# A graph-network edge pipeline on one core: t moves beside s in PSUM and lags z by a step, and the v picks are added as 128 columns

## The chip, the cores and the metric

One core of a Trainium2 chip. The time is the device time of one run of the kernel, in microseconds (us); the median of several runs counts.

## What is computed

The reference, cut to what matters. N = 6250 nodes, D = 64, E = 200,000 edges sorted by `dst`, NB = 8 basis values for each edge.

```python
h  = relu(layernorm(x))
p1 = tanh(h @ pp_W1 + pp_b1) @ pp_W2 + pp_b2
inter = concat(p1[src], p1[dst]) @ pi_W1 + pi_b1
inter = (inter @ pi_W2 + pi_b2) @ pi_W3              # [E, 64*8]
i1 = einsum('ecb,eb->ec', inter.reshape(E, 64, 8), edge_attr)
i1 = tanh(i1 @ ii_W1 + ii_b1) @ ii_W2 + ii_b2
out = x + segment_sum(i1, dst, 6250)
```

## The kernel before, in words

**Tables first.** A prologue of some 95 us makes two tables in HBM, `u_tab` (the part of `inter` that comes from `src`, fp32) and `v_tab` (the part from `dst`, as three bf16 pieces whose sum is the fp32 value), and folds the weights into `g_sb` and `w_out`.

**The edge loop.** Edges go in NG = 391 groups of 512 (4 tiles of 128). Since `dst` is sorted, a group's `dst` values lie in a window of W = 42 nodes. The branch `is_fast` holds this loop; the other branch isn't taken. A group g passes through these pieces of work:

- *gather*: POOL issues 4 indirect DMAs (L392) that bring 128 rows of `u_tab` each into `u_rows`, a ring of UR = 8 groups. Before group g it waits until `s_ready` has counted group g-8, whose slot it takes (L390).
- *window and places*: SP issues two DMAs, `loc_bc` (L334, place of each edge in the window, sent to 126 partitions) and `v_win` (L338, 42 rows of `v_tab` as 126 partitions), rings of VR = 4. L338 waits for `s_ready` of group g-4, L334 for `hot_t_ready` of group g-4.
- *hot_t* (DVE, L765): one-hot of the places, 126 x 512, bf16.
- *s* (PE): `place_rows` (L1017) transposes the gathered rows into `s_ps` (bank 4 or 5, 256 columns of fp32, alternating), and `add_v` (L1025) adds v by two matmuls of 64 weight columns (`v_win`), one for each half of the 128 partitions (`TWICE[j]`), 256 moving columns each. It ends with `s_ready`.
- *st* (ACT, L538): 4 activations copy `s_ps` to `st_sb` (`st_ready`).
- *spread* (PE, L1033): 16 matmuls of 24 rows spread the basis values into `spread_ps` (banks 0 to 3, `spread_ready`).
- *products* (DVE, L697): `o_sb` = st times spread, 128 x 2048 in one instruction (`o_ready`).
- *z* (PE, `z_group`, L1041): 8 fp32 matmuls of 64 weight columns, 256 moving columns (16 records), into bank 6 columns 0 to 255 (`z_ready`).
- *tanh* (ACT, L526): `z_ps` to `tt_sb` (`tt_ready`).
- *t* (PE, `t_transposes`, L1048): two fp32 transposes of `tt_sb` into `t_ps`, bank 6 columns 256 to 511 (`t_ps_ready`).
- *copy_t* (ACT, L529): `t_ps` to `t_sb`, 2 buffers (`t_ready`).
- *hot* (DVE, L818): one-hot, 128 x 168, ring HR = 4.
- *seg* (PE, L1085): 4 fp32 matmuls of 65 weight columns and 42 moving ones into bank 7 (`seg_ready`).
- *add* (DVE, L795): bank 7 is added into the window of `acc_all` (`acc_done`).

An epilogue of some 25 us multiplies `acc` by `w_out`, adds x and stores.

**The order is written out by hand.** In step n the engines do, in this order:

- PE (`step`, a loop over 8 unrolled steps): s(n), spread(n-1), z(n-2), seg(n-3), t(n-2). z(n-2) waits for `t_ready` of group n-3, since z and t share bank 6 (L1077). t(n-2) waits for `tt_ready` of the same group (L1089).
- ACT: st(n), tanh(n-2), copy_t(n-2).
- DVE: add(n-4), in some steps a part of the basis split (L723 to L736), `places` (L757) or `turn` (L745), then hot_t(n+1), hot(n-2), products(n-1).
- POOL: 4 gathers of group n+8 as soon as s(n) frees their slot. SP: the two window DMAs.

ACT, DVE, POOL and SP run fully unrolled programs.

Of the kernel before, what the change touches and what calls it, by code (L numbers as in the profile page):

```python
# [8 lines left out]
def program(nc, x, src, dst, edge_attr, pp_W1, pp_b1, pp_W2, pp_b2, pi_W1, pi_b1, pi_W2, pi_b2, pi_W3,  # L9
# [53 lines left out]
    with ctx:  # L63
# [31 lines left out]
        u_rows = sb("u_rows", [P, UR, TILES, D])  # L95
        v_win = sb("v_win", [3 * W, VR, D], bf16)
        loc_bc = sb("loc_bc", [P, VR, GE], bf16)
# [53 lines left out]
        s_ps = [bank[4][:, 0:2 * P], bank[5][:, 0:2 * P]]  # L151
        z_ps, t_ps = bank[6][:, 0:2 * P], bank[6][:, 2 * P:2 * P + TILES * D]
        seg_ps = bank[7][0:D + 1, 0:W]
# [103 lines left out]
        def has(g):  # L257
            return 0 <= g < NG
# [3 lines left out]
        def _(sp):  # L262
# [57 lines left out]
            with sp.If(is_fast):  # L320
                for n in range(NG):
                    if has(n):
# [13 lines left out]
                        if g >= VR:  # L336
                            sp.wait_ge(s_ready, g - VR + 1)
                        sp.dma_start(v_win[:, g % VR, :], v_tab[bass.ds(start, W), :, :].rearrange("n w d -> w n d")  # L338
                                     ).then_inc(v_in[g % VR], 16)
# [17 lines left out]
        def _(pool):  # L357
# [13 lines left out]
            nc.gpsimd.memset(b_parts[:], 0.0)  # L371
            nc.gpsimd.memset(t_sb[:], 1.0)
            nc.gpsimd.memset(basis[:, FULL * NBT:], 0.0)
            nc.gpsimd.memset(src_e[:, FULL * TILES:], 0)
# [41 lines left out]
        def _(act):  # L416
# [111 lines left out]
            def copy_t(r):  # L528
                return nc.scalar.copy(t_sb[:, r, :, 0:D].rearrange("p (h q) c -> p q h c", h=2),  # L529
                                      t_ps.rearrange("p (q h c) -> p q h c", q=2, h=2))  # L530

# [10 lines left out]
            with act.If(is_fast):  # L542
                for n in STEPS:
                    if has(n):
                        act.wait_ge(s_ready, n + 1)
                        if has(n - 2):
                            act.wait_ge(o_ready, n - 1)
                        copy_st(n % 2).then_inc(st_ready, 1)
                    if has(n - 2):
                        g = n - 2  # L550
                        act.wait_ge(z_ready, g + 1)
                        if g >= 2:
                            act.wait_ge(t_ps_ready, g - 1)
                        tanh_z(g % 2).then_inc(tt_ready, 1)
                        act.wait_ge(t_ps_ready, g + 1)
                        if g >= 2:
                            act.wait_ge(seg_ready, g - 1)
                        copy_t(g % 2).then_inc(t_ready, 1)
            with act.Else():
# [11 lines left out]
        def _(dve):  # L571
# [203 lines left out]
            with dve.If(is_fast):  # L775
# [9 lines left out]
                for n in STEPS:  # L785
                    if n == 4:
                        dve.wait_ge(acc_zero, 1)
                    if has(n - 4):
                        g = n - 4
                        start = dve.value_load(base_row[0:1, g:g + 1], min_val=0, max_val=N - W)  # L790
# [100 lines left out]
        def _(pe):  # L891
# [130 lines left out]
            def add_v(u):  # L1022
                picks = hot_t[:, u % 2, :].rearrange("w (q j p) -> w j q p", q=2, j=2)
                for j in range(2):
                    last = nc.tensor.matmul(s_ps[u % 2][TWICE[j], :].rearrange("k (q p) -> k q p", q=2),  # L1025
                                            v_win[:, u % VR, :], picks[:, j], start=False, stop=True)
                return last
# [18 lines left out]
            def t_transposes(r):  # L1046
                for q in range(2):
                    last = nc.tensor.transpose(t_ps[:, q * P:(q + 1) * P], tt_sb[:, r, q * P:(q + 1) * P], ident[:])  # L1048
                return last

            def step(n, u, first, last_pass):
# [8 lines left out]
                if of(0):  # L1060
                    if of(2):
                        pe.wait_ge(st_ready, seen(2))
                    pe.wait_ge(u_in[u], n * (64 // UR) + 64)
                    place_rows(u_rows[:, u, :, :], u % 2, False)
                    pe.wait_ge(v_in[u % VR], n * (16 // VR) + 16 * (u // VR + 1))
                    pe.wait_ge(hot_t_ready, seen(0))
                    add_v(u).then_inc(s_ready, 1)
                if of(1):
                    if (u - 1) % BT == 0:
# [4 lines left out]
                if of(2):  # L1074
                    pe.wait_ge(o_ready, seen(2))
                    if of(3):
                        pe.wait_ge(t_ready, seen(3))  # L1077
                    z_group(u % 2).then_inc(z_ready, 1)
                if of(3):
                    pe.wait_ge(t_ready, seen(3))  # L1080
                    pe.wait_ge(hot_ready, seen(3))
                    if of(4):
                        pe.wait_ge(acc_done, seen(4))
                    for j in range(TILES):
                        last = nc.tensor.matmul(seg_ps, t_sb[:, (u - 3) % 2, j, :], hot[:, (u - 3) % HR, j, :],  # L1085
                                                start=(j == 0), stop=(j == TILES - 1))
                    last.then_inc(seg_ready, 1)
                if of(2):
                    pe.wait_ge(tt_ready, seen(2))  # L1089
                    t_transposes(u % 2).then_inc(t_ps_ready, 1)  # L1090

# [59 lines left out]
```

## Time and profile before

| what | value |
|---|---|
| three runs: median (lowest to highest) | 2601.27 us (2601.23 to 2613.06) |
| the profiled execution: its own time / its span | 2618.32 us / 2616.5 us |
| mean granted TensorE clock, share of 2.4 GHz | 0.814 |
| busy: PE, weight loads, DVE, ACT, POOL | 71%, 45%, 53%, 41%, 58% |
| DMA | 125.86 MB, 48 GB/s |

The span is what the trace shows from the first to the last instruction, and 1.8 us of the execution's own time lie outside it. A matmul's start is recorded and its end is modelled, so the time at which another engine is released tells when a matmul was really known to be complete. "remote" as releaser means that a wait ended by a semaphore for which the profile found no instruction that had ended just before.

### The profile page before, as it was taken

How to read it: one execution, taken by the hardware profiler on the slowest of the kernel's cores; microseconds unless marked ns; L12 is line 12 of the kernel's file. 1: busy time of each engine (PE TensorE's matmuls, PEld its weight loads, DVE VectorE, ACT ScalarE, POOL GpSimd, SP SyncE). 2: the span in 40 equal slices, each digit the busy share in tenths (PEclk: the TensorE clock that was granted, in tenths of full speed). 3: DMA queues.
4: the chain of work that ended last, by engine and by line, in shares of the span. 5: the costliest groups of instructions: out<-in, count | busy, mean ns of one | idle time of the engine just before them, and what ended most of it. 6: DMA issues, size and time to landing. Idle time of an engine off the chain costs nothing.

```text
span 2616.5 us, 52109 instructions
## 1 busy us (share of the span) xinstructions
PE 1864.1 (71%) x18378; PEld 1177.1 (45%) x18378; DVE 1383.5 (53%) x2286; ACT 1070.9 (41%) x2409; POOL 1521.1 (58%) x1581
## 2 busy tenths in 40 slices
PE   4277777677777767767677767777777767777777
PEld 3144444444444444444444444444444444444445
DVE  5354555555555545545555555455455554555555
ACT  4144444344444444444444444444444433444444
POOL 2666566566566665565666566666556655566660
PEclk8578878888778788788887887887777877887878
DMA  3322222222222222222222122222222122222221
GB/s 104 68 49 46 47 49 43 47 49 45 48 43 48 48 46 48 46 44 48 48 45 49 43 48 48 46 48 49 44 46 50 43 48 41 48 45 43 45 44 38
DMA packets 311278, 125.86 MB, mean 48 GB/s; under 512 B 233399, under 2 KB 283433, under 8 KB 311161
## 3 DMA queue, kind: packets, MB, share of 16 engines
q1 hardware_dynamic: 259985, 73.19, 14.1%
q0 software_dynamic: 50048, 51.35, 10.4%
q14 instruction: 105, 0.86, 0.1%
q10 hardware_dynamic: 1128, 0.26, 0.1%
q8 instruction: 12, 0.20, 0.0%
HBM read 118.67 MB, written 6.00 MB: 48 GB/s over the span
## 4 chain that ended last, share of the span: by engine, by line
PE 59%; issue 16%; another core or an unknown queue 14%; ACT 7%; DVE 2%; SPq 1%; ACTq 0%; DVEq 0%; DMA 0%
PE bank L1041 34%; PE bank L1048 6%; PE bank L1085 6%; PE spread_ps L1033 4%; PE bank L1025 4%; ACT st_sb L538 4%; PE bank L1017 3%; ACT tt_sb L526 2%; DVE o_sb L697 1%; SPq L277 0%; ACT t_sb L529 0%; PE spread_ps L1125 0%; PE bank L921 0%; DMA v_tab<-acc_all 0%
## 5 line engine op out<-in xcount | busy, mean ns | idle before, releaser
L392 POOL DMA_INDIRECT u_rows<-u_tab,src_e x1564 | 1514.7, 968 | 1034.8 <-PE bank L1025 476.8
L1041 PE MATMUL bank<-o_sb,g_sb 128*64 128x256 f32 x6256 | 1025.7, 484 | 284.8 <-issue 232.2
L697 DVE TENSOR_TENSOR o_sb<-st_sb,spread_ps 128x2048 f32<-128x2048 f32 x391 | 891.3, 2280 | 234.5 <-PE spread_ps L1033 134.0
L1041 PEld LDWEIGHTS bank<-o_sb,g_sb 128*64 128x64 f32 x6256 | 569.8, 171 | 580.0 <-issue 458.5
L538 ACT ACTIVATE st_sb<-bank,s_bias 64x256 f32<-64x256 f32 x1564 | 734.1, 469 | 117.6 <-PE bank L1025 83.2
L795 DVE TENSOR_TENSOR acc_all<-acc_all,bank 65x42 f32 x391 | 76.1, 195 | 919.0 <-remote 640.3
L526 ACT ACTIVATE tt_sb<-bank,z_bias 128x256 f32<-128x256 f32 x391 | 185.5, 474 | 753.0 <-PE bank L1041 386.6
L1048 PE MATMUL bank<-ident,tt_sb 128*128 128x128 f32 x782 | 188.2, 326 | 366.7 <-ACT tt_sb L526 234.4
L529 ACT COPY t_sb<-bank 128x256 f32<-128x256 f32 x391 | 146.5, 375 | 618.8 <-remote 340.8
L1085 PEld LDWEIGHTS bank<-hot,t_sb 128*65 128x65 f32 x3128 | 247.5, 156 | 210.4 <-issue 209.5
L1085 PE MATMUL bank<-hot,t_sb 128*65 128x42 f32 x3128 | 298.0, 251 | 10.8 <-issue 10.2
L1048 PEld LDWEIGHTS bank<-ident,tt_sb 128*128 128x128 f32 x782 | 88.9, 157 | 405.9 <-ACT tt_sb L526 255.4
L1017 PE MATMUL bank<-ident,u_rows 128*128 128x128 f32 x782 | 171.7, 306 | 21.0 <-issue 17.1
L1033 PE MATMUL spread_ps<-bt_sb,spread 24*128 24x128 bf16 x6256 | 171.9, 232 | 7.0 <-DVE o_sb L697 4.8
L765 DVE TENSOR_SCALAR hot_t<-loc_bc,iota_p 126x512 bf16<-126x512 bf16 x391 | 148.6, 380 | 20.7 <-DMA loc_bc<-loc_tab 19.0
L1025 PE MATMUL bank<-hot_t,v_win 126*64 126x256 bf16 x782 | 127.4, 323 | 32.0 <-DMA v_win<-v_tab 27.8
L1033 PEld LDWEIGHTS spread_ps<-bt_sb,spread 24*128 24x128 bf16 x6256 | 98.5, 98 | 63.5 <-issue 19.2
L818 DVE TENSOR_TENSOR hot<-loc_e,iota_f 128x168 f32<-128x168 f32 x391 | 125.6, 321 | 0.0
L1017 PEld LDWEIGHTS bank<-ident,u_rows 128*128 128x128 f32 x782 | 109.2, 158 | 32.0 <-issue 31.7
L1025 PEld LDWEIGHTS bank<-hot_t,v_win 126*64 126x64 bf16 x782 | 44.5, 111 | 110.4 <-issue 81.6
L757 DVE TENSOR_TENSOR loc_e<-dst_e,start_bc 32x16 f32<-32x16 int32 (+1 forms) x400 | 71.3, 178 | 8.7 <-issue 3.7
L745 DVE STREAM_TRANSPOSE bt_sb<-b_parts 128x512 bf16<-128x512 bf16 x98 | 68.8, 702 | 0.0
(109 smaller groups left out, 227.7 us busy)
## 6 DMA issues: line engine op xcount, KB each, us to landing
loc_bc<-loc_tab SPq DMA_DIRECT2D x391, 126.0 KB
u_rows<-u_tab,src_e POOLq DMA_INDIRECT x1564
v_win<-v_tab SPq DMA_DIRECT2D x391, 15.8 KB
basis<-edge_attr SPq DMA_DIRECT2D x24, 256.0 KB
v_tab<-acc_all SPq DMA_DIRECT2D x6, 375.0 KB
u_tab<-basis SPq DMA_DIRECT2D x6, 250.0 KB
out<-x_sb SPq DMA_DIRECT2D x2, 750.0 KB
x_sb<-x SPq DMA_DIRECT2D x3, 375.0 KB
```

What stands on the lines that cost most here:

```text
L392: pool.indirect_dma_start(out=u_rows[:, g % UR, j, :], out_offset=None, in_=u_tab[:, :], in_offset=bass.IndirectOffsetOnAxis(ap=src_e[:, g ...
L526: return nc.scalar.activation(tt_sb[:, r, :], z_ps, ACT.Tanh, bias=z_bias[:, 0:1])
L529: return nc.scalar.copy(t_sb[:, r, :, 0:D].rearrange("p (h q) c -> p q h c", h=2), t_ps.rearrange("p (q h c) -> p q h c", q=2, h=2))
L538: last = nc.scalar.activation(tiles[h * D:(h + 1) * D, j], s_ps[r][part].rearrange("p (q a e) -> p q a e", q=2, a=TILES), ACT.Identity, bi ...
L697: return nc.vector.tensor_tensor(o_sb[:, r, :, :].rearrange("p c (j e) -> p j c e", j=TILES), st_sb[:, r, :].rearrange("p (j e) -> p j e", ...
L765: nc.vector.tensor_scalar(hot_t[:, g % 2, :], loc_bc[0:3 * W, g % VR, :], iota_p[0:3 * W, 0:1], None, ALU.is_equal).then_inc(hot_t_ready, 1)
L1017: last = nc.tensor.matmul(s_ps[r][:, q * P:(q + 1) * P], rows[:, 2 * q:2 * q + 2, :].rearrange("p j k -> p (j k)"), ident[:], start=(q == ...
L1025: last = nc.tensor.matmul(s_ps[u % 2][TWICE[j], :].rearrange("k (q p) -> k q p", q=2), v_win[:, u % VR, :], picks[:, j], start=False, stop ...
L1033: last = nc.tensor.matmul(spread_ps[:, a, c * P:(c + 1) * P], spread[q, 2 * c:2 * c + 2, :].rearrange("p b k -> p (b k)"), bt_sb[q, r, :], ...
L1041: last = nc.tensor.matmul(z_ps[h * D:(h + 1) * D, 0:2 * P], g_sb[:, c, :], o_sb[:, r, c, 2 * h * P:(2 * h + 2) * P], start=(c == 0), stop= ...
L1048: last = nc.tensor.transpose(t_ps[:, q * P:(q + 1) * P], tt_sb[:, r, q * P:(q + 1) * P], ident[:])
L1085: last = nc.tensor.matmul(seg_ps, t_sb[:, (u - 3) % 2, j, :], hot[:, (u - 3) % HR, j, :], start=(j == 0), stop=(j == TILES - 1))
```

## The change

Three things change in the fast branch.

1. `t_ps` gets two buffers, in the upper 256 columns of banks 4 and 5, beside the two of s. It leaves bank 6 to z alone.
2. The order: PE does in step n s(n), t(n-3), seg(n-4), spread(n-1), z(n-2); ACT st(n), copy_t(n-3), tanh(n-2); DVE adds group n-5. z(n-2) now waits for `tt_ready` of group n-3 in place of `t_ready`. Since t(n-3) writes the bank from which st(n-1) was read, it waits for `st_ready` of n-1, and s(n) waits for `t_ready` of n-4 (the bank that copy_t read).
3. `v_win` is three times as wide, with zeros left and right of v (a memset of POOL in the prologue). `add_v` takes 128 weight columns, [v, 0] for one j and [0, v] for the other, and both matmuls write all 128 partitions.

```diff
-        v_win = sb("v_win", [3 * W, VR, D], bf16)
+        v_win = sb("v_win", [3 * W, VR, 3 * D], bf16)
-        z_ps, t_ps = bank[6][:, 0:2 * P], bank[6][:, 2 * P:2 * P + TILES * D]
+        z_ps = bank[6][:, 0:2 * P]
+        t_ps = [bank[4][:, 2 * P:4 * P], bank[5][:, 2 * P:4 * P]]
...
-                        sp.dma_start(v_win[:, g % VR, :], v_tab[bass.ds(start, W), :, :].rearrange("n w d -> w n d")
+                        sp.dma_start(v_win[:, g % VR, D:2 * D], v_tab[bass.ds(start, W), :, :].rearrange("n w d -> w n d")
...
+            nc.gpsimd.memset(v_win[:], 0.0)
...
+                    if has(n - 3):
+                        g = n - 3
+                        act.wait_ge(t_ps_ready, g + 1)
+                        if g >= 2:
+                            act.wait_ge(seg_ready, g - 1)
+                        copy_t(g % 2).then_inc(t_ready, 1)
                     if has(n - 2):
                         g = n - 2
                         act.wait_ge(z_ready, g + 1)
                         if g >= 2:
                             act.wait_ge(t_ps_ready, g - 1)
                         tanh_z(g % 2).then_inc(tt_ready, 1)
-                        act.wait_ge(t_ps_ready, g + 1)
-                        if g >= 2:
-                            act.wait_ge(seg_ready, g - 1)
-                        copy_t(g % 2).then_inc(t_ready, 1)
...
-                    if has(n - 4):
-                        g = n - 4
+                    if has(n - 5):
+                        g = n - 5
...
                 for j in range(2):
-                    last = nc.tensor.matmul(s_ps[u % 2][TWICE[j], :].rearrange("k (q p) -> k q p", q=2),
-                                            v_win[:, u % VR, :], picks[:, j], start=False, stop=True)
+                    last = nc.tensor.matmul(s_ps[u % 2].rearrange("k (q p) -> k q p", q=2),
+                                            v_win[:, u % VR, (1 - j) * D:(3 - j) * D], picks[:, j],
+                                            start=False, stop=(j == 1))
...
                 if of(0):
                     if of(2):
                         pe.wait_ge(st_ready, seen(2))
+                    if of(4):
+                        pe.wait_ge(t_ready, seen(4))
...
+                if of(3):
+                    pe.wait_ge(tt_ready, seen(3))
+                    if of(1):
+                        pe.wait_ge(st_ready, seen(1))
+                    if of(5):
+                        pe.wait_ge(t_ready, seen(5))
+                    t_transposes((u - 3) % 2).then_inc(t_ps_ready, 1)
+                if of(4):
+                    pe.wait_ge(t_ready, seen(4))
+                    pe.wait_ge(hot_ready, seen(4))
+                    if of(5):
+                        pe.wait_ge(acc_done, seen(5))
+                    for j in range(TILES):
+                        last = nc.tensor.matmul(seg_ps, t_sb[:, (u - 4) % 2, j, :], hot[:, (u - 4) % HR, j, :],
+                                                start=(j == 0), stop=(j == TILES - 1))
+                    last.then_inc(seg_ready, 1)
...
                 if of(2):
                     pe.wait_ge(o_ready, seen(2))
                     if of(3):
-                        pe.wait_ge(t_ready, seen(3))
+                        pe.wait_ge(tt_ready, seen(3))
                     z_group(u % 2).then_inc(z_ready, 1)
-                if of(3):
...
-                if of(2):
-                    pe.wait_ge(tt_ready, seen(2))
-                    t_transposes(u % 2).then_inc(t_ps_ready, 1)
```

## Rows read from the trace of the kernel before

**Rows 1.** The page: busy time of the engines, and the chain that ended last.

```profile
PE 1864.1 (71%) x18378; PEld 1177.1 (45%) x18378; DVE 1383.5 (53%) x2286; ACT 1070.9 (41%) x2409; POOL 1521.1 (58%) x1581
...
PE 59%; issue 16%; another core or an unknown queue 14%; ACT 7%; DVE 2%; SPq 1%; ACTq 0%; DVEq 0%; DMA 0%
```

**Rows 2.** The waits: engine, line, releaser, us in total, times, longest.

```profile
DVE acc_all L795 <- remote: 640.3, 214, 4.1
POOL u_rows L392 <- PE bank L1025: 476.8, 264, 7.9
...
ACT t_sb L529 <- remote: 340.8, 138, 3.2
...
PE bank L1048 <- ACT tt_sb L526: 234.4, 160, 7.4
...
PE bank L1041 <- ACT t_sb L529: 52.0, 45, 2.5
```

**Rows 3.** One line's duration (ns min/median/max), first and last start, by line.

```profile
L1041 PE MATMUL bank<-o_sb,g_sb x6256: 379/379/690, 106.5 to 2592.5; 128*64 128x256 f32 x196
...
L392 POOL DMA_INDIRECT u_rows<-u_tab,src_e x1564: 939/945/2692, 50.1 to 2556.1; - x196
```

**Rows 4.** Timeline of a plain step: start, us, engine, line, count, idle before and releaser.

```profile
1428.12 1.92 ACT L538 ACTIVATE st_sb<-bank,s_bias 64x256 f32<-64x256 f32 x4
1428.14 0.95 POOL L392 DMA_INDIRECT u_rows<-u_tab,src_e  x1 [1.46 <-remote]
1428.37 1.95 PE L1041 MATMUL bank<-o_sb,g_sb 128*64 128x256 f32 x16 [1.71 <-issue]
...
1428.63 2.27 DVE L697 TENSOR_TENSOR o_sb<-st_sb,spread_ps 128x2048 f32<-128x2048 f32 x1
1429.39 0.94 POOL L392 DMA_INDIRECT u_rows<-u_tab,src_e  x1 [0.30 <-issue]
...
1430.24 0.67 PE L1085 MATMUL bank<-hot,t_sb 128*65 128x42 f32 x8
...
1431.77 0.47 ACT L526 ACTIVATE tt_sb<-bank,z_bias 128x256 f32<-128x256 f32 x1 [1.73 <-PE bank L1041]
1431.89 0.94 POOL L392 DMA_INDIRECT u_rows<-u_tab,src_e  x1 [0.30 <-issue]
1432.30 0.44 PE L1048 MATMUL bank<-ident,tt_sb 128*128 128x128 f32 x2 [1.39 <-issue]
1432.85 0.43 PE L1017 MATMUL bank<-ident,u_rows 128*128 128x128 f32 x2
1433.21 0.30 PE L1025 MATMUL bank<-hot_t,v_win 126*64 126x256 bf16 x2
1433.44 0.40 PE L1033 MATMUL spread_ps<-bt_sb,spread 24*128 24x128 bf16 x16
1434.01 0.37 ACT L529 COPY t_sb<-bank 128x256 f32<-128x256 f32 x1 [1.77 <-PE bank L1048]
1434.14 0.20 DVE L795 TENSOR_TENSOR acc_all<-acc_all,bank 65x42 f32 x1 [3.24 <-remote]
...
1434.31 0.95 POOL L392 DMA_INDIRECT u_rows<-u_tab,src_e  x1 [1.47 <-PE bank L1025]
```

**Rows 5.** Timeline where POOL issues eight gathers without a pause.

```profile
1484.30 1.22 POOL L392 DMA_INDIRECT u_rows<-u_tab,src_e  x1 [1.94 <-PE bank L1025]
...
1487.63 1.95 PE L1041 MATMUL bank<-o_sb,g_sb 128*64 128x256 f32 x16
...
1493.64 0.94 POOL L392 DMA_INDIRECT u_rows<-u_tab,src_e  x1 [0.30 <-issue]
1496.06 0.47 ACT L526 ACTIVATE tt_sb<-bank,z_bias 128x256 f32<-128x256 f32 x1 [6.18 <-remote]
```

**Rows 6.** Busy time by stretch: us, engines' busy us (instructions), clock, DMA share, GB/s.

```profile
1483.90:1487.60 3.70, 3.64 (x46) 2.37 (x46) 3.61 (x7) 2.62 (x7) 2.69 (x3) 1.00 0.18 40
1487.60:1498.50 10.90, 4.62 (x54) 2.81 (x46) 4.18 (x6) 3.12 (x7) 5.62 (x7) 0.85 0.16 37
...
1612.30:1620.30 8.00, 6.64 (x46) 4.06 (x46) 6.29 (x21) 2.92 (x7) 3.77 (x5) 0.50 0.21 44
```

**Rows 7.** Groups by line: engine, shapes, count, busy us, mean ns, idle before.

```profile
L1025 PE MATMUL bank<-hot_t,v_win 126*64 126x256 bf16 x782 | 127.4, 323 | 32.0 <-DMA v_win<-v_tab 27.8 <-DVE hot_t L765 4.2
...
L371 POOL MEMSET b_parts<- 128x4096 bf16 x1 | 3.5, 3507 | 0.0
```

More of the change, by code:

```diff
@@ L529, in copy_t @@
                 return nc.scalar.copy(t_sb[:, r, :, 0:D].rearrange("p (h q) c -> p q h c", h=2),
-                                      t_ps.rearrange("p (q h c) -> p q h c", q=2, h=2))
+                                      t_ps[r].rearrange("p (q h c) -> p q h c", q=2, h=2))
             def copy_st(r):
@@ L785, in _ @@
                 for n in STEPS:
-                    if n == 4:
+                    if n == 5:
                         dve.wait_ge(acc_zero, 1)
-                    if has(n - 4):
-                        g = n - 4
+                    if has(n - 5):
+                        g = n - 5
                         start = dve.value_load(base_row[0:1, g:g + 1], min_val=0, max_val=N - W)
@@ L1047, in t_transposes @@
                 for q in range(2):
-                    last = nc.tensor.transpose(t_ps[:, q * P:(q + 1) * P], tt_sb[:, r, q * P:(q + 1) * P], ident[:])
+                    last = nc.tensor.transpose(t_ps[r][:, q * P:(q + 1) * P], tt_sb[:, r, q * P:(q + 1) * P], ident[:])
                 return last
@@ L1076, in step @@
                     if of(3):
-                        pe.wait_ge(t_ready, seen(3))
+                        pe.wait_ge(tt_ready, seen(3))
                     z_group(u % 2).then_inc(z_ready, 1)
-                if of(3):
[L1080 to L1087, printed above, removed]
-                if of(2):
-                    pe.wait_ge(tt_ready, seen(2))
-                    t_transposes(u % 2).then_inc(t_ps_ready, 1)
             with pe.If(is_fast):
```

## The prediction

> **What bounds the kernel now.** I read the page first [rows 1]. No engine is full: PE 71%, POOL 58%, DVE 53%. The chain that ended last holds 14% of releases from nowhere. So the bound is a ring of waits, and the waits tell which [rows 2]. The largest come from PE to others (DVE's add 640 us, ACT's copy_t 341 us, both "remote"), then POOL waiting 477 us for s. PE's own wait for copy_t, the one that the change removes, is only 52 us in total.
>
> Then the length of a step: the records of z start between 106.5 and 2592.5 [rows 3], 390 steps of (2592.5-106.5)/390 = 6.37 us. Prologue and epilogue are the other 131 us of the span.
>
> Then one plain step [rows 4], and what it shows decides this prediction. seg is recorded from 1430.24 and should be over by 1430.91, but DVE's add, which waits for nothing else, starts at 1434.14, after 3.24 us of idle time. t is recorded over at 1432.74, copy_t starts at 1434.01. s and spread, issued after them, are released within the same 0.3 us. So the completions of seg, t, s and spread reach the other engines in one bunch, and the bunch comes 2.1 us after the start of the group's fourth gather (1431.89). POOL then sees s and starts the next four at 1434.31. Hence the ring: s released, four gathers 1.25 us apart (1428.14 to 1431.89), 2.1 us to the bunch, 0.3 us to POOL's restart: 3.75+2.1+0.3 = 6.15, against 1434.31-1428.14 = 6.17. Where POOL issues eight gathers in a row [rows 5] it is starker: z, recorded from 1487.63 for 1.95 us, is seen by tanh at 1496.06, 2.4 us after the start of the last gather (1493.64). The same step done while POOL paused took 3.70 us [rows 6]. I take it that gathers in flight hold back the news of finished matmuls; the trace shows the coincidence in every plain step I read (over half of the steps lie between 6.05 and 6.35 us), not the cause.
>
> **The change, part by part.** The sum is made against the profiled execution, 2618.3 us; the median of the runs is 17 us lower, and I take those off at the end.
>
> *copy_t out of z's way.* Now z starts at 1428.37, after copy_t's 0.37 us and some 0.15 us of hops [rows 4]. Afterwards z(n-2) waits for products(n-2) and tanh(n-3), both done by then, so it can follow spread directly at 1433.84 in place of 1434.44: up to 0.6 us a step earlier. If nothing held the news, that is at most 0.6x390 = 234 us. In a plain step it is worth nothing by itself: the ring of the gathers doesn't pass through z. z is then finished early in the gathers' next batch, when news still passes.
>
> *t and seg a step later.* t(n-2) used to wait for tanh right behind seg; now s(n+1) lies in between, some 0.7 us of work (L1017 and L1025) [rows 4]. Queued behind the waiting t are now seg, spread and z; before, t had s, spread and z behind it. s escapes, so POOL's and SP's DMAs hang on t no longer. That is the real gain: s(n+1) can be done about 2.9 us after the bunch. It needs copy_t(n-3), which on ACT lies behind st(n): 1.92+0.37 [rows 4], then s itself, 0.43+0.30 less overlap. Seen early, it lets POOL go on to eight gathers without pause. Eight gathers with their tail took 9.3+2.4 us, with the restart 12.0 for two steps: 6.0 each [rows 5]. So plain steps go from 6.17 to between 6.0 and 6.17.
>
> *The long steps.* The mean, 6.37, is above the plain step, since steps at half clock take 8.0 us (granted 0.50) and a step after a hurried one 10.9, 14.6 for the pair against 2x6.17 [rows 6]. They are made by PE's own order (z, tanh, t, s in series), so these are where the 0.6 us and s's freedom help. I take the mean down to about 6.10: below the plain step's 6.17, above the 6.0 of double batches. That is 0.27x390 = -105 us. Bounds: 0 and 0.37 us (6.37 to 6.0), 144 us.
>
> *add_v with 128 columns.* The two matmuls of 297 to 323 ns lie almost on each other today, 0.30 us for both [rows 4, 7], since each has half of the columns. Side by side no more, they take up to a second 0.30 less overlap; nearest row: 16 z records at 0.12 us each for 256 columns. I take +0.11 us of PE a step, covered by the held bunch (PE idles 1.71 us before z). If that cover went, 0.11x390 = 43 us; below, nothing.
>
> By the Trainium skill, "TensorE: Matmul & The Clock Gate", Part 3, matmuls on distinct column groups run concurrently, and 128 columns give that up; the rows agree with it.
>
> *Waits added.* t(n-3) waits for st(n-1), over one step earlier; s(n) for copy_t(n-4), done 3.5 us earlier or more in the plain step, but the tight one if ACT is late. DVE's add a step later: it had 3.24 us of idle time ahead [rows 4], nothing. One more step to drain at the end: +4 us (the 3.70 of the hurried step, [rows 6]). The memset on POOL: 768 elements at 3507 ns for 4096 [rows 7] is 0.7 us, under POOL's wait in the prologue (first gather at 50.1, [rows 3]). SP issues as many DMAs of the same pieces.
>
> Sum: 2618.3-105+4 = 2517, less 17: **2500 us**.
>
> **The rivals.**
>
> *A. The news isn't held by the gathers.* Then only engines and true waits bind: POOL needs 4x1.25 = 5.0 us a step, PE 3.7 and DVE 3.6 [rows 6]. The floor: 390x5.0 = 1950, and 131, and 2: 2083, less 17: about 2066; with some idle at half clock 2150. For it: one step did run in 3.70 us. Against it: that was when POOL paused, and the bunches keep step with the fourth gather, not with PE's work. Chance 0.13.
>
> By the Trainium skill, "SBUF — State Buffer", Who interferes with whom, PE and ACT never wait on anyone, DMA included; by that rule this rival's time would come out. Rows 5, with 6.18 us of held z, speak against reading it so.
>
> *B. No difference.* s(n+1) is seen only with the bunch, POOL's ring stays at 6.17, and half-clock steps stay long. What is gained in z is lost in the same wait. 2595 to 2610. Chance 0.15.
>
> *C. Slower: tanh behind st and copy_t, with spread and z behind t.* On ACT tanh(n-2) now lies behind st(n) and copy_t(n-3), and on PE spread(n) and z(n-1) lie behind t(n-2). If z's news comes with the bunch, the chain is st 1.92, copy_t 0.37, tanh 0.47, t 0.44, seg 0.67, spread 0.40, z 1.95 = 6.2 us, as long as the ring [rows 4]. At half clock PE's part (3.46) is nearly twice that, 6.1 to 6.9, and the chain 8.9 to 9.7 against 8.0 today [rows 6]. The mean clock of 0.814 says that some 0.37 of the time is at half clock. Then (0.9 to 1.7)x0.37 = 0.33 to 0.6 us a step: +130 to +240, 2730 to 2840; half of that if only part of these steps are hit, 2670. It decides where z's news is later than copy_t's end. For it: z's news did come with the bunch in rows 5. Against it: in the plain step tanh started 3.4 us after z's start, before the bunch. Chance 0.28.
>
> **How the numbers follow.** My forecast, a modest gain, has 0.44. Faster by over 0.5%: 0.44 less 0.02 for its edge, plus 0.13 for A: 0.55. Within 0.5% (what a measurement of this kernel can tell from no change): 0.16. Slower: 0.29. The forecast's own range is 2450 to 2590. To hold 8 in 10 I go down towards A without holding its floor (2300), and up through B and most of C (2710).
>
> **What would show it.** Right: z starts with no wait for copy_t (the 52 us are gone); copy_t and add still start in a bunch about 2.1 us after a group's last gather; more runs of eight gathers; a mean step near 6.1. Wrong towards A: POOL's wait for s falls to nearly nothing and steps reach 5.0 us. Wrong towards C: PE waits longer ahead of L1048, now with spread late behind it, and POOL's wait for s grows above 477 us.

## The result, and the profile after

| kernel | median us (lowest to highest), runs | ratio to before, 95% interval |
|---|---|---|
| before | 2603.14 (2601.23 to 2613.06), 4 | |
| after | 2711.26 (2709.42 to 2720.29), 4 | 1.0414 [1.0379, 1.045] |

The change costs 108 us. The forecast of 2500 us had the wrong sign; the time lies just above the range's end of 2710, between the half and the full price of rival C. The profiled execution of after took 2720.29 us.

The page of after, busy time and chain, beside [rows 1]:

```profile
PE 1917.7 (71%) x18378; PEld 1189.0 (44%) x18378; DVE 1361.3 (50%) x2286; ACT 1089.9 (40%) x2409; POOL 1517.3 (56%) x1582
...
another core or an unknown queue 38%; issue 20%; DVE 18%; PE 15%; DVEq 4%; ACT 3%; SPq 1%; ACTq 0%; DMA 0%
```

No engine does more that matters (PE +54 us, at nearly the same mean clock, 0.82). What grew is the share of the chain whose releaser the profile can't name, 14% to 38%, and DVE's, 2% to 18%. One line's duration, first and last start, beside [rows 3]:

```profile
L1047 PE MATMUL bank<-o_sb,g_sb x6256: 376/379/689, 105.0 to 2694.0; 128*64 128x256 f32 x196
```

z is now L1047, and a step takes (2694.0-105.0)/390 = 6.64 us against 6.37. From the first z to the last, after takes 2589.0 us and before 2486.0: 103 us more, which is all of the 102 us between the two profiled executions. The waits of after, beside [rows 2]:

```profile
DVE o_sb L702 <- remote: 1145.2, 324, 8.2
ACT tt_sb L529 <- remote: 629.8, 194, 6.5
...
PE bank L1054 <- ACT tt_sb L529: 502.1, 250, 4.7
POOL u_rows L395 <- PE bank L1030: 514.1, 227, 5.6
...
ACT st_sb L541 <- DVE o_sb L702: 285.1, 254, 1.9
```

DVE no longer waits in its add but in its products (L702), for spread: 1145 us in 324 steps. PE's wait for tanh ahead of t doubled, from 234 to 502 us. The groups by line of after (busy us, mean ns, idle us before) for seg (L1089), copy_t (L532), add (L800) and add_v (L1030):

```profile
L1089 PE MATMUL bank<-hot,t_sb 128*65 128x42 f32 x3128 | 301.8, 256 | 188.2 <-DVE acc_all L800 179.6 <-issue 0.3
...
L532 ACT COPY t_sb<-bank 128x256 f32<-128x256 f32 x391 | 146.9, 376 | 11.0 <-PE bank L1054 1.6
...
L800 DVE TENSOR_TENSOR acc_all<-acc_all,bank 65x42 f32 x391 | 73.4, 188 | 4.9 <-PE bank L1089 4.9
...
L1030 PE MATMUL bank<-hot_t,v_win 126*128 126x256 bf16 x782 | 165.8, 296 | 34.8 <-DMA v_win<-v_tab 27.8
```

The add (L800) had 640 us of remote wait ahead of it before [rows 2]; now it starts with none, because what it adds is ready long before DVE comes to it, and PE's seg waits 180 us for it instead. A step of after in its timeline (t is L1054, seg L1089, spread L1039, z L1047, s L1022 and L1030):

```profile
1415.57 0.40 PE L1039 MATMUL spread_ps<-bt_sb,spread 24*128 24x128 bf16 x16
...
1417.99 0.95 POOL L395 DMA_INDIRECT u_rows<-u_tab,src_e  x1 [0.30 <-issue]
...
1420.04 2.29 DVE L702 TENSOR_TENSOR o_sb<-st_sb,spread_ps 128x2048 f32<-128x2048 f32 x1 [3.49 <-remote]
1420.10 0.47 ACT L529 ACTIVATE tt_sb<-bank,z_bias 128x256 f32<-128x256 f32 x1 [2.95 <-remote]
...
1420.63 0.44 PE L1054 MATMUL bank<-ident,tt_sb 128*128 128x128 f32 x2 [2.19 <-ACT tt_sb L529]
...
1422.24 0.19 DVE L800 TENSOR_TENSOR acc_all<-acc_all,bank 65x42 f32 x1
...
1422.58 0.64 PE L1089 MATMUL bank<-hot,t_sb 128*65 128x42 f32 x8 [1.51 <-DVE acc_all L800]
...
1423.15 0.57 PE L1039 MATMUL spread_ps<-bt_sb,spread 24*128 24x128 bf16 x16
...
1423.65 3.42 PE L1047 MATMUL bank<-o_sb,g_sb 128*64 128x256 f32 x16
...
1426.26 2.29 DVE L702 TENSOR_TENSOR o_sb<-st_sb,spread_ps 128x2048 f32<-128x2048 f32 x1 [3.32 <-remote]
...
1426.99 0.44 PE L1022 MATMUL bank<-ident,u_rows 128*128 128x128 f32 x2
...
1428.40 0.97 POOL L395 DMA_INDIRECT u_rows<-u_tab,src_e  x1 [3.31 <-PE bank L1030]
```

Read it from the bunch at 1420.04, 2.05 us after the start of the last gather (1417.99), as in the kernel before. Spread, over at 1415.97, comes out only there, and so does z (tanh starts at 1420.10, with ACT idle for 2.95 us). From here PE works in its new order: t waits for tanh, seg waits for the add, the add stands on DVE behind products' 2.29 us, and only behind seg come spread (1423.15) and z (1423.65). In the kernel before, spread was done ahead of the bunch and z stood first behind it [rows 4]. So the next s comes late: it starts at 1426.99, 6.95 us after the bunch, and POOL, done with its four gathers, idles for 3.31 us up to 1428.40. Spread, over at 1423.72, is again seen only with the next bunch at 1426.26, so the next products start late too, and the loop closes.

Part of the length of this step is the clock: it was granted at 0.76 of full speed from 1420.04 to 1426.26, and z takes 3.42 us in place of 1.95. A step of the kernel before with z as slow is the fair one to hold beside it. These are its z and the s behind it:

```profile
1434.44 3.27 PE L1041 MATMUL bank<-o_sb,g_sb 128*64 128x256 f32 x16 [0.59 <-issue]
...
1438.55 0.38 PE L1017 MATMUL bank<-ident,u_rows 128*128 128x128 f32 x2
```

There s starts 4.54 us after copy_t showed the bunch (1434.01), 2.4 us sooner than in after.

### The profile page after: what moved, and what is told of

The parts are those of the page before. It is cut to its first block, busy times and chain, and to the rows that moved or that the text cites. A ratio compares the mean times of both kernels' runs of the same rounds, so it can differ in the third digit from the quotient of the medians.

```text
span 2718.5 us, 52595 instructions
## 1 busy us (share of the span) xinstructions
PE 1917.7 (71%) x18378; PEld 1189.0 (44%) x18378; DVE 1361.3 (50%) x2286; ACT 1089.9 (40%) x2409; POOL 1517.3 (56%) x1582
## 4 chain that ended last, share of the span: by engine, by line
another core or an unknown queue 38%; issue 20%; DVE 18%; PE 15%; DVEq 4%; ACT 3%; SPq 1%; ACTq 0%; DMA 0%
PE bank L1047 6%; DVE o_sb L702 5%; DVE hot_t L770 3%; PE spread_ps L1039 3%; PE bank L1089 2%; DVE hot L823 2%; DVEq L795 2%; DVE loc_e L762 2%; DVE acc_all L800 2%; ACT st_sb L541 2%; DVE bt_sb L750 2%; PE bank L1054 1%; PE bank L1022 1%; ACT tt_sb L529 1%
## 5 line engine op out<-in xcount | busy, mean ns | idle before, releaser
L702 DVE TENSOR_TENSOR o_sb<-st_sb,spread_ps 128x2048 f32<-128x2048 f32 x391 | 894.4, 2287 | 1276.6 <-remote 1145.2
L1047 PE MATMUL bank<-o_sb,g_sb 128*64 128x256 f32 x6256 | 1020.4, 482 | 1.9 <-issue 1.8
L1047 PEld LDWEIGHTS bank<-o_sb,g_sb 128*64 128x64 f32 x6256 | 518.7, 172 | 342.0 <-issue 216.5
L1054 PE MATMUL bank<-ident,tt_sb 128*128 128x128 f32 x782 | 190.0, 329 | 525.6 <-ACT tt_sb L529 502.1
L1089 PE MATMUL bank<-hot,t_sb 128*65 128x42 f32 x3128 | 301.8, 256 | 188.2 <-DVE acc_all L800 179.6
L1089 PEld LDWEIGHTS bank<-hot,t_sb 128*65 128x65 f32 x3128 | 277.0, 167 | 246.1 <-issue 244.8
L1054 PEld LDWEIGHTS bank<-ident,tt_sb 128*128 128x128 f32 x782 | 95.0, 160 | 622.4 <-ACT tt_sb L529 523.1
L1022 PE MATMUL bank<-ident,u_rows 128*128 128x128 f32 x782 | 191.1, 330 | 16.3 <-issue 16.3
L1039 PE MATMUL spread_ps<-bt_sb,spread 24*128 24x128 bf16 x6256 | 189.6, 250 | 3.2 <-issue 3.2
L1030 PE MATMUL bank<-hot_t,v_win 126*128 126x256 bf16 x782 | 165.8, 296 | 34.8 <-DMA v_win<-v_tab 27.8
L1022 PEld LDWEIGHTS bank<-ident,u_rows 128*128 128x128 f32 x782 | 86.4, 154 | 204.2 <-issue 204.1
L532 ACT COPY t_sb<-bank 128x256 f32<-128x256 f32 x391 | 146.9, 376 | 11.0 <-PE bank L1054 1.6
L770 DVE TENSOR_SCALAR hot_t<-loc_bc,iota_p 126x512 bf16<-126x512 bf16 x391 | 137.4, 352 | 20.9 <-remote 17.5
L1039 PEld LDWEIGHTS spread_ps<-bt_sb,spread 24*128 24x128 bf16 x6256 | 108.0, 105 | 27.9 <-issue 4.4
L1030 PEld LDWEIGHTS bank<-hot_t,v_win 126*128 126x128 bf16 x782 | 82.7, 108 | 49.1 <-DMA v_win<-v_tab 28.1
L800 DVE TENSOR_TENSOR acc_all<-acc_all,bank 65x42 f32 x391 | 73.4, 188 | 4.9 <-PE bank L1089 4.9
```

The costliest lines, as they stand in the source:

```text
L702: return nc.vector.tensor_tensor(o_sb[:, r, :, :].rearrange("p c (j e) -> p j c e", j=TILES), st_sb[:, r, :].rearrange("p (j e) -> p j e", ...
L770: nc.vector.tensor_scalar(hot_t[:, g % 2, :], loc_bc[0:3 * W, g % VR, :], iota_p[0:3 * W, 0:1], None, ALU.is_equal).then_inc(hot_t_ready, 1)
L1022: last = nc.tensor.matmul(s_ps[r][:, q * P:(q + 1) * P], rows[:, 2 * q:2 * q + 2, :].rearrange("p j k -> p (j k)"), ident[:], start=(q == ...
L1030: last = nc.tensor.matmul(s_ps[u % 2].rearrange("k (q p) -> k q p", q=2), v_win[:, u % VR, (1 - j) * D:(3 - j) * D], picks[:, j], start=Fa ...
L1039: last = nc.tensor.matmul(spread_ps[:, a, c * P:(c + 1) * P], spread[q, 2 * c:2 * c + 2, :].rearrange("p b k -> p (b k)"), bt_sb[q, r, :], ...
L1047: last = nc.tensor.matmul(z_ps[h * D:(h + 1) * D, 0:2 * P], g_sb[:, c, :], o_sb[:, r, c, 2 * h * P:(2 * h + 2) * P], start=(c == 0), stop= ...
```

## The experiments

There are five sets of runs (the recorded expectations say "call"). The kernels of a set ran on one chip, and each is compared with the kernel before in the same set. In the first, third and fourth set the kernel before took 2611, 2614 and 2612 us; in the second and fifth it took 2063. What differs between them is not known. The chip alone doesn't seem to decide it: the record numbers the chips 2, 15, 11, 10 and 11, so the third set (2614) and the fifth (2063) bear the same number.

**First set: the parts one by one** (before 2610.84 us). `b_v128` is the kernel before with the picks of v as 128 columns, the third point of the change alone. `a_v64` is the kernel after with that point undone:

```diff
-                    last = nc.tensor.matmul(s_ps[u % 2].rearrange("k (q p) -> k q p", q=2),
-                                            v_win[:, u % VR, (1 - j) * D:(3 - j) * D], picks[:, j],
-                                            start=False, stop=(j == 1))
+                    last = nc.tensor.matmul(s_ps[u % 2][TWICE[j], :].rearrange("k (q p) -> k q p", q=2),
+                                            v_win[:, u % VR, :], picks[:, j], start=False, stop=True)
```

`a_spread_first` and `a_seg_last` are the kernel after with one piece of PE's `step` moved:

```diff
# after:           s, t, seg, spread, z
# a_spread_first:  s, spread, t, seg, z
# a_seg_last:      s, t, spread, z, seg
```

> The kernel before with the third part of the change alone (wide v_win, 128 weight columns). If the order of PE's work is what cost 108 us (my theory), this costs nothing to 15 us: 2600 to 2618. If the picks on 128 columns are what cost (rival: 0.1 to 0.3 us of PE a step, uncovered), it is 2640 to 2710.

> The changed kernel with v_win narrow and the picks on twice 64 columns again; t stays beside s and the order stays. Order theory: 2690 to 2711, since s lies on the chain of a step now and gets 0.05 us shorter. Rival (the picks cost): down to 2600 to 2640.

> The changed kernel with one move on PE: s(n), spread(n-1), t(n-3), seg(n-4), z(n-2). spread no longer stands behind t, which waits for tanh, nor behind seg, which waits for DVE's add. Order theory: spread is released in the same bunch as the s before it, products start a bunch earlier in the chain, the step falls from 6.64 to 6.2 to 6.4 us: 2540 to 2630. If what costs is z standing behind t and seg with s behind z, not spread: little changes, 2680 to 2711. If ACT's order (tanh behind st and copy_t) is the cause: no change, 2711.

> The changed kernel with seg(n-4) moved behind z(n-2): s(n), t(n-3), spread(n-1), z(n-2), seg(n-4). It takes seg's 0.64 us and its wait for DVE's add (180 us in all) out of the chain in front of spread and z, and puts 0.64 us between z and s. Order theory: the wait of 180 us goes, some of it is left as a shorter chain, 0.1 to 0.5 us a step: 2520 to 2670. If t's wait for tanh alone makes the step: no change, 2690 to 2711.

Measured:

| kernel | median us | ratio to before, 95% interval |
|---|---|---|
| b_v128 | 2618.39 | 1.003 [1.0015, 1.0046] |
| a_v64 | 2722.74 | 1.0422 [1.0394, 1.045] |
| a_spread_first | 2567.20 | 0.9825 [0.9802, 0.9848] |
| a_seg_last | 2601.16 | 0.9963 [0.9948, 0.9977] |

The two moves on PE came out as the order theory said (2540 to 2630 and 2520 to 2670 expected). b_v128 and a_v64 lie 0.4 and 12 us above their ranges; the kernel before was 8 us slower here than in the first result.

The picks are not it: 8 us in the order before, and in the order after nothing that shows (a_v64 has the ratio 1.0422, after itself 1.0414 to 1.0446 in three measurements). The order on PE carries the loss. The five pieces, their buffers and the orders of ACT and DVE are the same in the last two kernels as in after, and they are 1.8% and 0.4% faster than before. After wasn't run in this set, so a_v64 stands for it: moving seg behind z gives 2722.7-2601.2 = 122 us, and moving spread ahead of t gives 2722.7-2567.2 = 156 us with seg left where it was. These are two ways of breaking one loop, and not two parts of a sum. Moving t alone wasn't tried. Groups by line of a_spread_first (seg is L1095 there), then of a_seg_last (seg is L1100):

```profile
L1095 PE MATMUL bank<-hot,t_sb 128*65 128x42 f32 x3128 | 290.9, 252 | 0.6 <-DVE acc_all L800 0.6
...
L702 DVE TENSOR_TENSOR o_sb<-st_sb,spread_ps 128x2048 f32<-128x2048 f32 x391 | 894.5, 2288 | 1084.3 <-PE spread_ps L1039 638.8 <-remote 439.2 <-PE bank L1047 5.9
```

```profile
L1100 PE MATMUL bank<-hot,t_sb 128*65 128x42 f32 x3128 | 301.1, 252 | 17.3 <-issue 16.6 <-DVE acc_all L800 0.6
```

The 180 us of seg's wait for the add are 0.6 in both, though the add stands as late in DVE's program as in after. A step of a_spread_first shows why:

```profile
1415.63 2.29 DVE L702 TENSOR_TENSOR o_sb<-st_sb,spread_ps 128x2048 f32<-128x2048 f32 x1 [3.13 <-PE spread_ps L1039]
...
1416.12 0.62 PE L1095 MATMUL bank<-hot,t_sb 128*65 128x42 f32 x8
1416.66 1.95 PE L1047 MATMUL bank<-o_sb,g_sb 128*64 128x256 f32 x16
...
1417.94 0.20 DVE L800 TENSOR_TENSOR acc_all<-acc_all,bank 65x42 f32 x1
```

Here, too, products start with the bunch and the add stands behind them. But spread went ahead of t on PE, so these are the products of one group later, and seg needs only the add before them, which is done. seg and z follow without waiting.

**Second set: what holds the news** (before 2063.38 us). Three cuts of the kernel before, and the order s, spread, t, z, seg with the narrow picks:

```diff
# b_half: two of the four gathers
-                    for j in range(TILES):
+                    for j in range(2):
# b_direct: no gather, one plain DMA of SP per group
+                        sp.dma_start(u_rows[:, g % UR, :, :], u_tab[0:GE, :].rearrange("(p j) d -> p j d", j=TILES)
+                                     ).then_inc(u_in[g % UR], 16)
# b_noloc: loc_bc for the first four groups only
+                        if g < VR:
```

> The kernel before with two of the four gathers of a group (tiles 2 and 3 of u_rows stay zero, so half of the edges lack their u part). Theory (news of finished matmuls waits for the gathers in flight): the ring is 1.25+2.1+0.3 = 3.65 us, other limits take over, the step falls from 6.37 to 4.2 to 5.0 us: 1750 to 2080. Rival (the news is late for another reason, POOL isn't a bound, it is busy 58% of the time): the step stays: 2560 to 2610.

> The kernel before with no indirect DMA: SP brings 512 consecutive rows of u_tab a group by one plain DMA, the same bytes into the same ring (the rows are the wrong ones, so the sums are wrong). Theory (POOL's indirect DMAs hold the news): no late bunch, step 4.0 to 4.8 us: 1700 to 2000. Rival (any DMA that writes u_rows at this rate holds it): 2400 to 2610.

> The kernel before in which SP sends loc_bc for the first four groups alone (later groups use the places of those). It takes out the largest DMA of a step, 126 KB. Theory: the ring of the gathers stays, 2560 to 2620. Rival (the window's DMA holds the news, whose packets move just when z is late): down to 2100 to 2400.

> Both moves together and v_win narrow: PE does s(n), spread(n-1), t(n-3), z(n-2), seg(n-4), picks on twice 64 columns. The run with spread first is at 6.25 us a step, 0.1 above the ring of the gathers (6.15). Theory: the ring can't be undercut by another order: 2545 to 2575. Rival (a chain through seg or add_v is left in it): 2450 to 2540.

Measured: b_half 1624.94, b_direct 1617.1, b_noloc 2050.61 us (one run each), a_mix 2056.42, ratio 0.9966 [0.9953, 0.9978]. The expectations were written for a kernel before of about 2605 us and can't be judged here, since before took 2063. The timeline of a_mix (z is L1045 there) says why:

```profile
804.79 0.94 POOL L394 DMA_INDIRECT u_rows<-u_tab,src_e  x1 [0.30 <-issue]
...
805.90 1.95 PE L1045 MATMUL bank<-o_sb,g_sb 128*64 128x256 f32 x16
806.04 0.94 POOL L394 DMA_INDIRECT u_rows<-u_tab,src_e  x1 [0.30 <-issue]
...
807.29 0.94 POOL L394 DMA_INDIRECT u_rows<-u_tab,src_e  x1 [0.30 <-issue]
...
807.89 0.47 ACT L528 ACTIVATE tt_sb<-bank,z_bias 128x256 f32<-128x256 f32 x1 [0.28 <-PE bank L1045]
```

The gathers are 1.25 us apart without an end, and yet z, over by 807.85, is seen by tanh at 807.89. In this set no news is held, POOL waits for PE 1.8 us in the whole run, and four gathers set a step of 5.0 us. That is rival A, whose floor was put at 2066. b_noloc asked whether the DMA of `loc_bc` holds the news; it wasn't run where before takes 2611, so that question stays open but for b_direct2 below, which keeps this DMA.

**Third set: the same cuts where news is held** (before 2614.03 us).

> The kernel after once more, beside the kernel before in the same call, because the kernel before takes about 2605 us in some calls and 2063 us in another, where finished matmuls are told of at once and POOL's four gathers of 1.25 us set the step (5.0 us). Theory A (the order on PE costs time only because one bunch of late news comes per step): where before takes about 2605 us, after is at 2711 again, ratio 1.04; where before takes about 2063 us, after's PE order also fits into 5.0 us, so ratio 0.99 to 1.01. Rival B (spread and z behind t cost a fixed 0.27 us per step, whoever sets the step): ratio 1.04 in either, so 2063 becomes 2150 to 2170.

> The kernel before with two of each group's four gathers (the other rows of u stay zero: half of the u picks are left out). The same edit gave 1625 us in a call where the kernel before took 2063. If before takes about 2605 here: theory A (news is held while gathers are in flight, until about 2 us after the last one) gives a bunch per 1.25 + 2.1 + 0.3 = 3.65 us of POOL's ring, but PE's own work of 3.7 us per step and a bunch that can't hold all of it bring 4.0 to 5.0 us per step: 1670 to 2060. Rival B (news is late on that chip whatever POOL does) leaves 2300 or more. If before takes about 2063: 1620 to 1630 again.

> The kernel before with u_rows loaded by one plain transfer from SP per group in place of four gathers from POOL (the rows are not the picked ones: the picks of u are left out). The same edit gave 1617 us in a call where the kernel before took 2063. If before takes about 2605 here: theory A (gathers hold the news) gives the same 1600 to 1650, since no gather is left. Rival B (any transfer, or the chip itself, holds it) gives 1900 or more. If before takes about 2063: 1610 to 1625 again.

> The kernel after with two of each group's four gathers (half of the u picks are left out), beside the same edit of the kernel before. Theory A (after's order costs time only through late news): if before takes about 2063 here, a_half is within 1% of b_half (1625), since PE's work of 3.7 us per step sets both; if before takes about 2605, a_half is slower than b_half by 2 to 6%. Rival B (the order itself costs): a_half is 60 to 130 us above b_half in either case.

Measured: after_again 2729.96, ratio 1.0446 [1.0419, 1.0472]; b_half2 1910.92; b_direct2 1619.18; a_half 2020.48 (the last three one run each). This set is of the other kind, and it ties the hold to the gathers: without them the kernel takes 1619 us here and 1617 where before takes 2063, though all its other DMAs are still there and SP moves the bytes of `u_rows`. With two gathers it takes 1911 against 1625. The clock isn't the reason: its mean is 0.974 and 0.976 in these two. So the two kinds of set differ only while gathers are issued. A step of b_half2 (z is L1042):

```profile
1410.55 1.95 PE L1042 MATMUL bank<-o_sb,g_sb 128*64 128x256 f32 x16
1410.56 0.94 POOL L393 DMA_INDIRECT u_rows<-u_tab,src_e  x1 [2.46 <-PE bank L1026]
1411.27 2.29 DVE L698 TENSOR_TENSOR o_sb<-st_sb,spread_ps 128x2048 f32<-128x2048 f32 x1 [0.98 <-PE spread_ps L1034]
1411.81 0.94 POOL L393 DMA_INDIRECT u_rows<-u_tab,src_e  x1 [0.30 <-issue]
...
1413.44 0.47 ACT L527 ACTIVATE tt_sb<-bank,z_bias 128x256 f32<-128x256 f32 x1 [1.21 <-PE bank L1042]
1413.71 0.20 DVE L796 TENSOR_TENSOR acc_all<-acc_all,bank 65x42 f32 x1 [0.15 <-PE bank L1086]
```

z was over at 1412.50 and is seen at 1413.44, 1.63 us after the start of the second gather; after one gather some news gets through earlier (products at 1411.27, 0.71 us behind it). a_half is 5.7% above b_half2: with fewer gathers, too, the order after loses where news is held. It wasn't run where before takes 2063, where the expectation has it level.

**Fourth set: a second window for the news** (before 2611.96 us). POOL pauses between the second and the third gather of each group:

```diff
                     for j in range(TILES):
+                        if j == 2:
+                            if g:
+                                pool.wait_ge(gap_done, g)
+                            nc.gpsimd.memset(gap[:], 0.0).then_inc(gap_done, 1)
```

> The kernel after once more. Where the kernel before takes about 2610 us in this call: ratio 1.04 again by every theory. Where it takes about 2063 (news at once, POOL's gathers set the step of 5.0 us): theory A (order costs only through late news) 0.99 to 1.01; rival B (t, seg ahead of spread and z cost by themselves) 1.03 or more.

> The kernel after with spread ahead of t, seg and z on PE, once more. Where before takes about 2610: ratio 0.98 again. Where before takes about 2063: theory A 0.99 to 1.00, since the four gathers of 1.25 us set the step in all orders; rival B 0.98 there too.

> The kernel before with a memset of 128x1024 f32 (about 1.0 us by the 529 ns of 128x520) on POOL between the second and third gather of each group; nothing is left out. Where before takes about 2610: the ring of POOL grows by the 1.0 us if the hold after the last gather stays 2.1 us: 391 more us, 3000; if a run of two gathers holds the news 1.6 us only (as in b_half2), 2800. If the news came at its own pace between gathers and the pause only moves it, 2610 to 2700. Where before takes about 2063: 2063 + 391 = 2450.

> The kernel after with the same pause. Theory A (after loses because spread's and z's news misses the step's one bunch): the pause lets a second bunch out in each step, so a_gap is within 1% of b_gap although after is 4% above before. Rival B (the order costs by itself, or the news isn't let out by the pause): a_gap stays 3 to 5% above b_gap. Where before takes about 2063: equal to b_gap within 1% by A, 3% above by B.

Measured: after_third 2723.73, ratio 1.0423 [1.0387, 1.0459]; a_spread_first2 2565.23, ratio 0.9817 [0.9791, 0.9843]; b_gap 2838.72; a_gap 2659.32 (one run each). The ratios repeat. The pause was a surprise: I had put both kernels level, and they cross over. It costs the kernel before 227 us, and the kernel after, with 0.9 us more of POOL in each step, gets 64 us faster. In a_gap (spread is L1045, products L708):

```profile
1412.17 1.04 POOL L401 DMA_INDIRECT u_rows<-u_tab,src_e  x1 [0.30 <-issue]
...
1412.95 0.61 PE L1045 MATMUL spread_ps<-bt_sb,spread 24*128 24x128 bf16 x16
1413.21 0.96 POOL L400 MEMSET gap<- 128x1024 f32 x1
...
1413.91 2.29 DVE L708 TENSOR_TENSOR o_sb<-st_sb,spread_ps 128x2048 f32<-128x2048 f32 x1 [1.27 <-PE spread_ps L1045]
```

Spread, over at 1413.56, is seen in the pause at 1413.91, 1.74 us after the second gather, and products start there instead of with the bunch behind the fourth. In b_gap (t is L1054, s L1023 and L1031):

```profile
1412.24 0.94 POOL L398 DMA_INDIRECT u_rows<-u_tab,src_e  x1 [0.30 <-issue]
1414.09 0.47 ACT L532 ACTIVATE tt_sb<-bank,z_bias 128x256 f32<-128x256 f32 x1 [5.98 <-remote]
...
1414.62 0.69 PE L1054 MATMUL bank<-ident,tt_sb 128*128 128x128 f32 x2 [5.66 <-ACT tt_sb L532]
...
1415.09 0.63 PE L1023 MATMUL bank<-ident,u_rows 128*128 128x128 f32 x2
...
1416.36 0.95 POOL L398 DMA_INDIRECT u_rows<-u_tab,src_e  x1 [3.18 <-PE bank L1031]
```

There z's news comes last, t waits 5.66 us for it, s stands behind t, and POOL waits for s. That is just the chain which the change cuts: in its order s stands ahead of the waiting t. With the pause the kernel after is 2838.7-2659.3 = 179 us ahead (one run each). So the gain that was forecast for s shows here; how much of the 179 us is s alone was not tried.

**Fifth set: pauses again** (before 2062.63 us). `sf_gap` is a_spread_first with the pause, `a_gap_short` the kernel after with a memset a quarter as wide.

> The kernel after with spread ahead of t, seg and z on PE (2565 to 2567) and the pause of 1.0 us (memset of 128x1024 f32) on POOL between the second and third gather of each group. Theory A (in after, the pause gained 65 us because spread's news came out in it; with spread first there is nothing left to gain): 2650 to 2850, slower than without the pause by the pause's own cost, up to 391 us less what hides. Rival B (a pause lets any held news out, z's among them, and gains in every order but before's): 2480 to 2550.

> The kernel after with a pause of about 0.3 us (memset of 128x256 f32, which took 0.30 us in the kernel before) in the same place. Theory A (news comes out only if the next gather doesn't follow within about 1.6 to 2 us of the last): 0.3 us is too short, so no gain, and the ring is longer by 0.3 us: 2720 to 2840. Rival B (any slack after the second gather helps): 2600 to 2700.

Measured: sf_gap 2418.42, ratio 1.1731 [1.1711, 1.1751]; a_gap_short 2159.98, ratio 1.0483 [1.0461, 1.0506]. In this set nothing is held, so neither question on held news was answered. They show something else. POOL's groups in a_gap_short:

```profile
L401 POOL DMA_INDIRECT u_rows<-u_tab,src_e x1564 | 1519.1, 971 | 462.1 <-issue 419.3 <-DMA u_tab<-basis 41.8 <-PE bank L1036 1.1
...
L400 POOL MEMSET gap<- 128x256 f32 x391 | 133.3, 341 | 0.1
```

and in sf_gap:

```profile
L401 POOL DMA_INDIRECT u_rows<-u_tab,src_e x1564 | 1529.2, 978 | 460.9 <-issue 419.6 <-DMA u_tab<-basis 40.6 <-PE bank L1036 0.6
...
L400 POOL MEMSET gap<- 128x1024 f32 x391 | 379.3, 970 | 0.1
```

POOL waits for s 1.1 us in the whole run. Its own time, 1519.1+462.1+133.3 = 2115, lies 43 us under the span of 2158.0; in sf_gap 1529.2+460.9+379.3 = 2369, 46 us under 2415.5. Where nothing is held POOL's sum sets the time in both orders on PE. The kernel after without a pause wasn't run in such a set. With POOL waiting 1.1 us for its order even with the short pause, it should be within 1% of before there, as a_mix is (an estimate).

## Why the prediction was wrong

*The ring and the hold* were right. The bunch 2.1 us behind the last gather is in after too (1417.99 to 1420.04), and b_direct2 makes a cause of the coincidence where before takes 2614 us, by one run. *Rival A*, at 0.13, says that nothing is held; its floor of 2066 us is what the kernel before takes in the sets where that is so (2063). By the Trainium skill, "SBUF — State Buffer", Who interferes with whom, PE and ACT never wait on anyone. That section is about access to SBUF, and PE's own work agrees with it: z's 16 records take 1.95 us in a_mix and in b_half2. It doesn't say how soon another engine learns that they are over, and that is where the two differ (0.04 and 0.94 us).

*copy_t out of z's way*: the wait is gone, as said. It was larger than the 52 us that the prediction read, since z's row in before has 232 us more under "issue", and in [rows 4] z starts 0.14 us after copy_t is over. L1041 idled 284.8 us before and L1047 idles 1.9. But "it can follow spread directly at 1433.84" did not come. z does follow spread, only spread isn't there any more: it stands behind t and seg, at 1423.15, which is 3.1 us after the bunch.

*t and seg a step later* is the step that failed. The prediction names the queue behind the waiting t ("seg, spread and z") and then prices only s, which escapes; seg, spread and z behind t stand in the sum at nothing. With them there the mean step went from 6.37 to 6.64 us in place of 6.10, and moving spread alone ahead of t takes 156 us off, more than the whole loss. The same part says of s that it "can be done about 2.9 us after the bunch". In the step of after shown above it starts 6.95 us after it.

One zero in *Waits added* belongs to it: "DVE's add a step later: it had 3.24 us of idle time ahead, nothing." In a_spread_first the add is as late and costs nothing that shows. In after it does not hold, for the add stands behind products, which start only with the bunch since spread was late. It lets seg go at 1422.58, 2.5 us after the bunch, and seg in its turn holds spread and z. PE waits 180 us in all for the add. What that wait costs apart from seg's own 0.64 us in the queue was not tried: the 122 us of a_seg_last hold both. The prediction asked what the add waits for, and not who waits for the add.

*The long steps*: the mean went from 6.37 to 6.64 us, not to 6.10. A part of the forecast -105 us is there once spread goes ahead of t: a_spread_first makes (2542.3-106.1)/390 = 6.25 us a step, and takes 44 us less than before. Its z records:

```profile
L1047 PE MATMUL bank<-o_sb,g_sb x6256: 376/379/690, 106.1 to 2542.3; 128*64 128x256 f32 x196
```

*add_v*: forecast +0.11 us of PE a step, covered, 43 us if not. Measured (165.8-127.4)/391 = 0.10, and 8 us of time in the kernel before, nothing that shows in after. *Waits added to s and t* cost nothing that shows; no run tried them alone, nor POOL's memset. *The drain*, put at +4 us, hardly grew: from the last z to the end of the span it is 24.0 us before and 24.5 after.

*Rival C* had the right sign and half of the place: spread and z behind t, PE waiting longer ahead of t (234 to 502 us), POOL's wait for s up from 477 to 514. Its other half, tanh behind st and copy_t on ACT, did not happen: ACT was idle for 2.95 us when tanh was released, and copy_t waits 11.0 us in total. It has nothing of seg's wait for the add either. So its price came near by luck in part: 110 us above the 2601 us that it starts from, against 70 for its half and 130 for the whole, and some of that from a chain that isn't there.

The best of these orders where news is held, a_spread_first, beats both kernels: 2565 to 2567 us, 1.8% below before in two sets.

## What to carry to other kernels

When an instruction with a late wait moves forward in an in-order engine, price everything behind it up to the end of the loop, not only what escapes; and when a consumer moves a step later, look at what it releases, since idle time ahead of it is no slack for those that wait for it. Where finished work is announced in one bunch per step, a piece on whose news another engine's long work hangs, here spread, belongs ahead of the pieces that wait for other engines. In a_spread_first z still stands behind t and seg, so nothing here shows that z has to be early too.

## What the runs showed of the hardware

The same kernel took 2603 to 2614 us in some sets of runs and 2063 in others, a quarter more. The difference is tied to GpSimd's indirect DMAs: without them 1619 and 1617 us, with two per group 1911 and 1625, with four 2612 and 2063. Where it occurs, the completions of matmuls reach other engines some 1.6 us (two gathers) to 2.1 us (four) after the start of the last gather of a run. Why it occurs in one set and not in another stays open. The third and the fifth set bear the same chip number, 11, with 2614 and 2063 us, so the chip alone doesn't decide it, if the number names one chip both times.

Where matmuls are seen late, ACT and DVE are not. In [rows 4] tanh on ACT is over at 1432.24, with the fourth gather under way since 1431.89, and t on PE starts at 1432.30, 0.06 us later. So it is in all the 255 steps of that trace in which PE stood idle until tanh was over: t starts within 0.06 us. In the step of after shown above, DVE's add is over at 1422.43, with a gather under way since 1421.65, and seg starts at 1422.58.

A pause of 0.96 us on POOL made one kernel 2.4% faster (2723.7 to 2659.3, the latter one run), and the same pause made another one 8.7% slower (2612.0 to 2838.7, the latter one run).
